# A four-layer sequence model on one core: the hydra blocks' input transposed by DMA instead of TensorE, LayerNorm's epsilon on GpSimd, and a new order for every engine

## Time and profile before

| | |
|---|---|
| runs, median (lowest to highest) | 1409.86 us (1408.0 to 1412.52) |
| the profiled execution's own time | 1409.34 us |
| its span, first to last instruction | 1407.5 us |
| PE busy | 1330.7 us, 95% |
| DVE busy | 1030.7 us, 73% |
| ACT busy | 795.1 us, 56% |
| POOL busy | 766.2 us, 54% |

### The profile page before, as it was taken

The page is one execution under the profiler, slowest core; times in us unless marked ns, Lnnn a source line. Parts: engine busy times, 40 slices in busy tenths (PEclk is TensorE's granted clock), DMA queues, the critical chain, the costliest instruction groups (busy, mean ns, idle before and its releaser), DMA issues. The chain is left out here.

```text
span 1407.5 us, 32864 instructions
## 1 busy us (share of the span) xinstructions
PE 1330.7 (95%) x11934; PEld 978.2 (69%) x11934; DVE 1030.7 (73%) x2328; ACT 795.1 (56%) x1753; POOL 766.2 (54%) x963
## 2 busy tenths in 40 slices
PE   5788999989999999999999899999999999999998
PEld 2445866677678777868686667667777768586775
DVE  6988887876778889877777787968696778665121
ACT  3877787877687868877885244333424432331221
POOL 3656688688787577887544435254434434351221
PEclk8879999999999999999999999999999999999999
DMA  7573578578985554787662100641001000000000
GB/s 207 160 177 83 124 136 165 134 136 154 166 162 131 119 127 113 146 179 140 137 129 48 46 1 16 256 135 38 8 9 38 16 1 34 20 9 16 1 16 16
DMA packets 232356, 131.95 MB, mean 94 GB/s; under 512 B 151738, under 2 KB 215458, under 8 KB 231298
## 3 DMA queue, kind: packets, MB, share of 16 engines
q1 hardware_dynamic: 230956, 129.77, 39.9%
q10 hardware_dynamic: 1238, 0.07, 0.1%
HBM read 75.00 MB, written 19.92 MB: 67 GB/s over the span
## 5 line engine op out<-in xcount | busy, mean ns | idle before, releaser
L2004 PE MATMUL ps<-x3h,w1gu 128*128 128x256 f16 x1792 | 298.9, 273 | 3.4 <-DVE prod L1657 3.4
L1255 ACT ACTIVATE Pe<-ps,nmax 128x256 f32<-128x256 f32 (+3 forms) x512 | 252.8, 535 | 62.2 <-DVE nmax L1398 36.2
L1398 DVE TENSOR_REDUCE nmax<-ps 128x1 f32<-128x384 f32 (+3 forms) x352 | 222.7, 635 | 42.3 <-PE ps L1894 37.9
L2004 PE MATMUL ps<-x3l,w1gu 128*128 128x256 f16 x896 | 244.2, 273 | 0.0
L2004 PEld LDWEIGHTS ps<-x3h,w1gu 128*128 128x128 f16 x1792 | 175.3, 98 | 28.1 <-DVE prod L1657 5.0
L1393 DVE TENSOR_TENSOR pt<-ps,pt 128x512 f16<-128x512 f32 (+1 forms) x256 | 161.3, 632 | 34.8 <-ACT pt L1239 33.8
L1135 POOL TENSOR_TENSOR int1l<-prod,int1h 128x256 f16<-128x256 f32 x112 | 95.5, 858 | 137.1 <-ACT int1h L1354 137.1
L1239 ACT ACTIVATE pt<-ps 128x512 f16<-128x512 f32 (+1 forms) x256 | 143.3, 560 | 39.4 <-PE ps L1901 30.4
L1891 PE MATMUL ps<-kT,qT 128*128 128x256 f16 (+3 forms) x512 | 138.2, 305 | 16.0 <-ACT Pe L1255 15.0
L1901 PE MATMUL ps<-identf,Pe 128*128 128x128 f32 x928 | 148.0, 279 | 2.9 <-DVE pt L1393 2.0
L838 POOL TENSOR_TENSOR stp<-Pe,stp 128x512 f16<-128x512 f32 (+1 forms) x96 | 103.9, 1082 | 40.6 <-ACT stp L1247 40.5
(11 more groups left out here) (269 smaller groups left out, 3377.6 us busy)
## 6 DMA issues: line engine op xcount, KB each, us to landing
w1gu<-w_gu SPq DMA_DIRECT2D x7, 1024.0 KB, 8.1
x_dram<-xr SPq DMA_DIRECT2D x18, 256.0 KB, 3.1
xr<-in_x SPq DMA_DIRECT2D x16, 256.0 KB, 3.5
x2a<-x_dram SPq DMA_DIRECT2D x4, 1024.0 KB, 5.7
vq<-in_q1g SPq DMA_DIRECT2D x28, 128.0 KB, 2.5
vz<-in_z1g SPq DMA_DIRECT2D x28, 128.0 KB, 3.9
vs<-in_s1g SPq DMA_DIRECT2D x28, 128.0 KB, 4.6
w_gu<-vh SPq DMA_DIRECT2D x56, 64.0 KB, 2.3
```

The lines of the kernel that those rows point to most:

```text
L1255: ins = act.activation(Pe[:, u % 2, x * w:(x + 1) * w], ps[:, u % 2, x * w:(x + 1) * w], ACT.Exp, bias=nmax[:, u % 4, x:x + 1])
L1398: dve.tensor_reduce(nmax[:, u % 4, 0:g], ps[:, u % 2, 0:g * w].rearrange("p (g w) -> p g w", g=g), AX, ALU.max, negate=True).then_inc(sem( ...
L2004: ins = pe.matmul(ps[:, bank, piece * H2:piece * H2 + H2], w1gu[:, j // 2, 2 * piece + pw, k, cols], px[:, k, h * H2:h * H2 + H2], start=( ...
```

## The change

Four things change together.

1. **Way in.** `c1_tr` and `c1_te` go. GpSimd makes the two float16 halves of each tile (step `cs`: a copy and a subtract, 128x512 each), into buffers that have just come free (`halves_of`). SP issues one DMA transpose of the 1024 columns into `xTb` (step `cd`). `c1_dn` becomes 12 float16 matmuls of 128 columns. VectorE splits `w_down` once (in `consts_a`). The GELU's scale undoes the weight scale.
2. **Epsilon.** VectorE's L1374 goes; GpSimd adds epsilon itself, as one more instruction ahead of each of the 64 powers.
3. **Tile 3's low halves** move from GpSimd to VectorE (`LO_POOL`), 16 steps.
4. **Order.** New values for `MARGIN`, `WO_AT`, `CH0_AT`, `IN_AT`, `FFN0_AT`, new planned durations, and a rank `OUT_RANK` for the hydra layer's way out. All five lists come out anew.

```diff
-LO_POOL = (3, 6, 7, 12, 13, 14, 15)
+LO_POOL = (6, 7, 12, 13, 14, 15)
-        A("SP", "x2a", s, 3600, stored + ([("c1_tr", (s - 1, l)) for l in range(NB)] if s else staged(NT - 1)), R0)
+        A("SP", "x2a", s, 3600, stored + ([("c1_dn", (s - 1, l)) for l in range(NB)] if s else staged(NT - 1)), R0)
-            A("PE", "c1_tr", (s, l), 440, after, R0, takes=0 if s else 1)
-            A("ACT", "c1_te", (s, l), 620, [("c1_tr", (s, l)), ("c1_dn", (s, l - 2)) if l >= 2 else None], R0, frees=None if s else ("c1_tr", (s, l)))
-            A("PE", "c1_dn", (s, l), 900, [("c1_te", (s, l)), ("weights_a", 0), ("h_raw", 2 * s - 1) if s else None], R0, takes=0 if s or l else 1)
+            A("POOL", "cs", (s, l), 1900, [("x2a", s), ("consts_a", 0), ("mix", s - 2) if s > 1 else None], R0)
+            A("SP", "cd", (s, l), 2100, [("cs", (s, l)), ("c1_dn", (s, l - 2)) if l >= 2 else ("c1_dn", (s - 1, l + 2)) if s else None], R0)
+            A("PE", "c1_dn", (s, l), 690, [("cd", (s, l)), ("h_raw", 2 * s - 1) if s else None], R0, takes=0 if s or l else 1)
...
+OUT_RANK = (400, 406, 406, 400)
-MARGIN = {'pt': 1500, 'w1c': 1500, 'dq': 2500, 'dk': 2500, 'x_load': 2000, 'x1_load': 1500}
+MARGIN = {'cd': 1500, 'pt': 2500, 'w0': 1500, 'w1c': 3000, 'dq': 2500, 'dk': 2500, 'x_load': 2000, 'x1_load': 1500}
-WO_AT = 0
-CH0_AT = [-10 + 0.5 * c for c in range(NC0)]
+WO_AT = 4
+CH0_AT = [-9 + 0.75 * c for c in range(NC0)]
-IN_AT = [-20, -10] + [FIRST[t] - 24 for t in range(2, NT)]
-FFN0_AT = [(37, 162), (226, 520), (402, 467), (482, 717), (721, 889), (877, 907), (899, 904), (912, 982)]
+IN_AT = [-20, -10, 0, 44, 73, 72, 106, 120, 158, 178, 164, 190, 212, 232, 276, 296]
+FFN0_AT = [(69, 131), (181, 422), (332, 455), (455, 460), (422, 1112), (1097, 1206), (1146, 1322), (1284, 1365)]
...
+        def halves_of(s, l):
+            return (x2a[:, l - 1, :] if l else xmid[:, s % 2, :]).bitcast(F16)
...
+                if kind == "cd":
+                    s, l = key
+                    sp.wait_ge(sem("cs"), NB * s + l + 1)
+                    if s or l >= 2:
+                        sp.wait_ge(sem("c1_dn"), NB * s + l - 1)
+                    sp.dma_start_transpose(out=xTb[:, l % 2, :, :], in_=halves_of(s, l)).then_inc(sem(f"ld_cd{l % 2}"), 16)
...
+                if kind == "cs":
+                    s, l = key
+                    to = halves_of(s, l)
+                    if l == 0:
+                        pool.wait_ge(sem("ld_x2a"), 16 * (s + 1))
+                        pool.wait_ge(sem("alog"), 1)
+                        if s > 1:
+                            pool.wait_ge(sem("hT"), s - 1)
+                    if s or l:
+                        pool.wait_ge(sem("cs"), NB * s + l)
+                    own.link(pool.tensor_copy(to[:, 0:D], x2a[:, l, :]))
+                    pool.tensor_tensor(to[:, D:2 * D], x2a[:, l, :], to[:, 0:D], ALU.subtract).then_inc(sem("cs"), 1)
...
             own.link(dve.bn_stats(st[:, :], r))
-            dve.sem_inc(sem("bn"), 1)
-            own.link(dve.bn_aggr(m, st[:, :]))
-            dve.tensor_scalar(v, m[:, 1:2], EPS, None, ALU.add).then_inc(ready, 1)
+            dve.bn_aggr(m, st[:, :]).then_inc(ready, 1)
...
+                own.link(pool.tensor_scalar(r[:, o:o + 1], v[:, o, 1:2], 1.0, EPS, ALU.mult, ALU.add))
+                pool.tensor_tensor(r[:, o:o + 1], r[:, o:o + 1], neghalf[:, 0:1], ALU.pow).then_inc(sem(kind), 1)
...
                 for k in range(KD):
-                    ins = pe.matmul(ps[:, dn_bank(s), l * P:(l + 1) * P], wdT[:, k, :], xTb[:, l % 2, k, :], start=(k == 0), stop=(k == KD - 1))
+                    for at, (px, pw) in enumerate(((0, 0), (0, 1), (1, 0))):
+                        ins = pe.matmul(ps[:, dn_bank(s), l * P:(l + 1) * P], wd[pw][:, k, :], xTb[:, l % 2, px * KD + k, :],
+                                        start=(k == 0 and at == 0), stop=(k == KD - 1 and at == 2))
```

More of the change, by code:

```diff
@@ L383, in way_out @@
         A("DVE", "x1_sum", t, 690, [e], r, frees=("wo", t))
-        A("DVE", "bn1", t, 1300, [("x1_sum", t), ("x1", t - 2) if t >= 2 else None], r)
-        A("POOL", "rstd1", t, 600, [("bn1", t)], r - 4)
+        A("DVE", "bn1", t, 1050, [("x1_sum", t), ("x1", t - 2) if t >= 2 else None], r)
+        A("POOL", "rstd1", t, 850, [("bn1", t)], r - 4)
         A("DVE", "x1", t, 570, [("rstd1", t)], r - 4)
@@ L483, in hydra @@
         free = ("h_z", 2 * s + 2) if s < NI - 1 else None
-        A("DVE", "mix", s, 1300, [("h_u", 2 * s + 1)], R0)
+        RO = OUT_RANK[s]
+        A("DVE", "mix", s, 1300, [("h_u", 2 * s + 1)], RO)
         for l in range(NB):
[L486 to L493, removed]
+            A("PE", "up", (s, l), 860, [("mix", s), free, ("x3_sum", (s, l - 3)) if l >= 3 else None], RO)
+            A("DVE", "x3_sum", (s, l), 1600, [("up", (s, l)), ("x3ld", s)], RO)
+            A("DVE", "bn3", (s, l), 1250, [("x3_sum", (s, l))], RO)
+            A("POOL", "rstd3", (s, l), 850, [("bn3", (s, l))], RO)
+            A("DVE", "x3", (s, l), 800, [("rstd3", (s, l))], RO)
+            A("PE", "x3tr", (s, l), 440, [("x3", (s, l)), ("x3l", (s, l - 3)) if l >= 3 else ("x3_sum", (s, 3 if l == 0 else l))], RO)
+            A("ACT", "x3h", (s, l), 600, [("x3tr", (s, l)), ("f1_gu", (s - 1, l // 2, NJ1 - 1), 1) if s else None], RO)
+            A("DVE", "x3l", (s, l), 690, [("x3h", (s, l))], RO)
     def ffn1(self, f):
@@ L1130, in pool_stream @@
                     pool.wait_ge(sem("ve3"), NB * s + l + 1)
-                    pool.tensor_tensor(rstdc[:, l:l + 1], vec[:, l:l + 1], neghalf[:, 0:1], ALU.pow).then_inc(sem("rstd3"), 1)
+                    own.link(pool.tensor_scalar(rstdc[:, l:l + 1], mvc[:, l, 1:2], 1.0, EPS, ALU.mult, ALU.add))
+                    pool.tensor_tensor(rstdc[:, l:l + 1], rstdc[:, l:l + 1], neghalf[:, 0:1], ALU.pow).then_inc(sem("rstd3"), 1)
                 if kind == "f1_lo":
@@ L1137, in pool_stream @@
                     pool.wait_ge(sem("ve4"), key + 1)
-                    pool.tensor_tensor(rstdd[:, key % 2:key % 2 + 1], ved[:, key % 2:key % 2 + 1], neghalf[:, 0:1], ALU.pow).then_inc(sem("rstd4"), 1)
+                    own.link(pool.tensor_scalar(rstdd[:, key % 2:key % 2 + 1], mvd[:, key % 2, 1:2], 1.0, EPS, ALU.mult, ALU.add))
+                    pool.tensor_tensor(rstdd[:, key % 2:key % 2 + 1], rstdd[:, key % 2:key % 2 + 1], neghalf[:, 0:1], ALU.pow).then_inc(sem("rstd4"), 1)
         @block.gpsimd
@@ L1295, in act_stream @@
                     act.wait_ge(sem("alog"), 1)
[L1296 removed]
+                    act.activation(xmid[:, key % 2, :], ps[:, dn_bank(key), :], ACT.Gelu, bias=bdn[:, 0:1], scale=1.0 / WA_SCALE).then_inc(sem("xmid"), 1)
                 if kind == "c_exp":
@@ L1506, in dve_constants @@
                 own.link(dve.tensor_scalar(A8[:, :], A8[:, :], 80.0, None, ALU.min))
+                own.link(dve.tensor_scalar(wd[0][:, :, :].rearrange("p k n -> p (k n)"), wd_load, WA_SCALE, 0.0, ALU.mult, ALU.add))
+                own.link(dve.scalar_tensor_tensor(out=wd[1][:, :, :].rearrange("p k n -> p (k n)"), in0=wd_load, scalar=WA_SCALE,
+                                                  in1=wd[0][:, :, :].rearrange("p k n -> p (k n)"), op0=ALU.mult, op1=ALU.subtract))
                 own.link(dve.tensor_scalar(inw[0][:, :], inw_load, WA_SCALE, 0.0, ALU.mult, ALU.add))
```

70 lines of the change are left out of this document (22 added, 48 removed).

## The result

The changed kernel takes **1445.34 us** (median of 4 runs, 1443.47 to 1446.23) against 1409.01 (1408.0 to 1412.52) for the kernel before: ratio 1.0252, 95% interval 1.0236 to 1.0269. The forecast was 1397. Its profiled execution has a span of 1443.1 us, 35.6 more than before.

The account below looks back on a forecast made before the run. PE was taken as the bound from 930 us on, with PE and DVE both near theirs from 745. Sum: 1407.5 - 10.2 - 2 + 0.1 = 1395.4 us span, plus 1.84 gives 1397; own range 1391 to 1403, 8 in 10 within 1386 to 1408.

Parts of the forecast that it names:

- From 930 on, what PE has to do is the time: Last 470 us: PE idle only 2.9 us, so other engines' gains or losses count nothing until PE waits.
- After 930 there is hardly a stall to trade: Argument against the no-change rival (1408 us, chance 0.10): behind 930 saved PE time can hardly return as waits.
- PE idle for well over 14 us between 745 and 930: Sign that would show the forecast wrong, if DVE or GpSimd is what releases PE there.
- Term 4: All lists made anew: -2 us, a quarter of PE's 8.9 us waiting for exponentials; bounds -18 and +13.
- Rival A: New lists matter more than the work, cutting PE's idle time before 745: -18 instead of -2, 1383 us; chance 0.17.
- Term 1: PE's way in, 16 tiles: two-byte matmuls save 0.64 us a tile, -10.2 us; bounds -11.2 and -0.6.
- counts wholly: Stages 2 and 3 run behind 930, so their -5.1 us of PE work comes fully off the time.
- Term 2: Epsilon from DVE to GpSimd in 64 LayerNorms: 14 us less DVE time, +0.1 us on the end; bounds -4 and +1.
- Term 3: Tile 3's low halves: POOL loses 18.6 us, DVE gains 11.0; effect between -4 and +4, counted in term 4.
- Term 5: Way in's cost to others: POOL gains 32 us, ACT loses 16 copies; GELU of stage 0 at 737, needed at 746.8.
- Hidden: 0: Stage 0's later way in costs no time, covered by about 10 us before GELU is needed at 746.8.
- rival B: Hydra chain bounds 745 to 930: GELU(0) 7 us late, stage 1's `cs` blocking DVE up to 8; 1419 us, chance 0.12.

Follow-up runs that it names:

- e1: The changed kernel with OUT_RANK all 400 as its only change: 1416.88 us, ratio 1.0050 to the kernel before.
- e2: The kernel before with OUT_RANK (400, 406, 406, 400) as its only change: 1445.51 us, ratio 1.0258.
- e15: e1 without stage 0's split of the down weights, GpSimd halves and turned loads: 1416.28 us, ratio 1.0035.
- e3: The kernel before, lists untouched, with only epsilon moved from VectorE to GpSimd: 1408.1 us, ratio 0.9992.
- e6: The kernel before, on its own lists, with both the new way in and epsilon on GpSimd: 1415.31 us, ratio 1.0029.
- e13: e6 without VectorE's addition of the convolution's bias in the eight hydra blocks: 1411.84 us, ratio 1.0003.
- e4: The kernel before, on its own lists, with only the new way in: 1417.58 us, ratio 1.0053.
- e10: e6 without GpSimd making the halves of stage 0's four tiles: 1415.06 us, ratio 1.0022.
- e14: e6 without stage 0's split of the down weights, GpSimd halves and turned loads: 1412.73 us, ratio 1.0008.
- e17: e3 with other starting ranks in the planner, chosen so that attention ends sooner: 1403.10 us, ratio 0.9938.

## Why the prediction was wrong, step by step

**What bounds the kernel.** "From 930 on, what PE has to do is the time" is the step under the whole sum, and it failed. A PE that is busy for 467.10 of 470 us is full, but what fills it is layer 4's work, which only lies there because the lists hold enough of it until the next stage's input comes. When `x3tr` of stage 1 came 28.5 us later (1057.1 for 1028.6), the stock ran out. "After 930 there is hardly a stall to trade" read the absence of stalls as safety; it was a balance that the ranks had made. The prediction had named one sign of being wrong that came: PE idle for well over 14 us between 745 and 930, 24.2, released mostly by VectorE.

**Term 4, the new order** is the term of the sum that was mis-sized: -2 us, with +13 as the worst. It was priced from PE's idle time up to 745 alone; `OUT_RANK` stood in the diff and got no price. It is worth +28 in the changed kernel (e1), +35.5 on the old one (e2). The rows could have priced it: behind `up` of stage 1 stand two hydra blocks with the rank 405, each of some 55 to 75 us from one `in` to the next, on a VectorE that is busy for most of the time, and the last `x3_sum` is what `x3tr` waits for. With the rest of the lists attention ends 7 to 10 us later (changed kernel, e1, e15), of which the way in may hold a part, since on the old lists it goes with 4 to 7. Rival A, that the lists matter more than the work, had the right item, but the wrong sign and the wrong place: it looked ahead of 745.

**Term 1, the way in on PE.** The price was right: 24 of the new matmuls take 1.34 us (starts at 955.05 to 956.33, and one distance), 0.67 a tile where I had said 0.72, and from e3 to e6 PE's busy time falls by 9.5 us. A tile's first ones:

```profile
725.23 0.22 PE L1944 MATMUL ps<-xTb,wdh 128*128 128x128 f16 x1
725.28 0.22 PE L1944 MATMUL ps<-xTb,wdl 128*128 128x128 f16 x1
725.34 0.28 PE L1944 MATMUL ps<-xTb,wdh 128*128 128x128 f16 x2
725.45 0.22 PE L1944 MATMUL ps<-xTb,wdl 128*128 128x128 f16 x1
```

But "counts wholly" was wrong. The stretch from layer 4's start shrank by 0.8 us for 5.1 forecast and 4.3 saved (e3 to e6), because PE's idle time there grew by 3.5; stages 0 and 1 gave nothing that shows. What e13 adds is that some of it appears once VectorE is lighter too.

**Term 2, epsilon.** Right: no difference (e3). VectorE's busy time nevertheless rose by 26.4 us in the changed kernel where I had forecast -2. By instruction, the additions that went were 10.0 us (forecast 14), tile 3's low halves are 14.2 (forecast 11), the weights' split is 1.1, and some 21 us are the same instructions taking longer: the eight multiplies into `yy` (L1609) go from 14.1 to 21.7 us, those into `ty` (L1611) from 19.6 to 15.8. What lengthened them is not shown. GpSimd's rose by 19.8 (forecast 26), ScalarE's fell by 9.5 (forecast 9.6).

**Term 3, tile 3's low halves.** Not tested by itself; no run shows whether it lay within the ±4 that I gave it.

**Term 5, the costs for others.** "Hidden: 0" was wrong: e4 is 7 us slower than before, but the mechanism I had in mind, a GELU that comes too late for the hydra block, was not it. GELU(0) came at 741.95 (forecast 737), ahead of attention's end, as said. GpSimd's `cs` and the turned loads cost little (ratios 0.0007 lower in e10 and 0.0021 in e14, 1 and 3 us). What I had not priced is that the later GELU holds a bank of PSUM until 742 (2.3 us in e14), and that PE waits longer for attention's exponentials (0.7 us in e3, 4.6 in e6, 2.7 in e14).

GpSimd's subtract of `cs` took what the forecast said (the copy 0.61 us for 0.81), and in the changed kernel was hardly held up:

```profile
L1131 POOL TENSOR_TENSOR x2a<-x2a x12: 1154/1156/1378, 720.4 to 1019.9; 128x512 f16<-128x512 f32 x12
L1131 POOL TENSOR_TENSOR xmid<-x2a,xmid x4: 1153/1161/1542, 716.9 to 1006.7; 128x512 f16<-128x512 f32 x4
```

The longest is 0.4 us over the median; in e6 one subtract took 2.14 us and the copy before it 1.74. These two ran from 766.15 to 770.11, beside VectorE's `yc` (L1598 and L1599, 765.57 to 769.10); the other 15 copies took 0.61 each. VectorE was held up beside `cs` as well: in e6 `sm_e` (L1594) took 1.15 us for a median of 0.19, from 761.01 to the end of a subtract (760.92 to 762.12), and in the changed kernel `ty` (L1574) took 1.23 for a median of 0.42, from 910.41 on beside the subtract of 910.20 to 911.36. But rival B's price of up to 8 us for stage 1's `cs` did not appear. In e6 these `cs` run at 755.9 to 770.1 beside stage 0's chain, which takes 117.1 us from its `in` to stage 1's (757.2 to 874.3), 118.4 in e3 (752.9 to 871.4). From there to stage 3's `in` it is 260.6 and 261.4 us.

**Rival B** said that the chain becomes the bound between 745 and 930. It had the sign right, with a chance of 0.12, and forecast 1419. The chain did decide, but through its start (attention's end) and, some 100 us behind 930, through the rank of the way out, not through GpSimd.

What stays open: why PE waits longer for attention's exponentials in e4, e6 and still in e14, how e1's later end divides between its lists and the way in, and what lengthened VectorE's instructions.

## What to carry to other kernels

A fully busy engine under a fixed order is not yet the bound: ask what keeps it supplied, how long the stock lasts, and which step on another engine brings the next input. In a diff, price every change of priority first, by what can now stand in front of that step; here one number, 406 instead of 400, was worth 28 us against the 10 us of arithmetic that I had priced with care. And when work is taken from an engine, look for the point that starts the chain (here attention's end): in e17 moving it by 10.0 us moved the last matmul by 9.1, while the 4.3 us saved behind it gave 0.8.

## What the runs showed of the hardware

- PE stopped at 1043 for 14.2 us. Its granted clock was 0.95 in 1042 to 1046, 0.50 in 1046 to 1066 and 0.99 in 1066 to 1070, so it stayed at 0.50 for 9 us after work had come back at 1057. The wait cost more than its length: behind layer 4's start PE is busy 4.1 us longer than in e1 for as many matmuls (3724 and 3723).
- In the changed kernel the float16 matmuls of 128 columns (L1944, 192 of them with 192 weight loads) start every 0.056 us in a row; the record of each says 0.22. 24 of them took PE 1.34 us, a quarter of the 5.3 that their records add up to: the distance from start to start gives what they cost, the record's length does not.
- In the changed kernel the 16 DMA transposes of 128x1024 halves (`xTb`, L1000) held SP for 1.24 us in the median and landed 2.7 to 7.6 us after issue, half of them by 2.8; the slowest held SP for 3.68 us.
- The kernel before had medians of 1409.0 to 1411.9 us at the five times it was measured, so a difference under 0.2% says nothing without the kernel before measured beside it.
